# Decoder layer on one core: fp16 pairs for every projection, q and k transposed by DMA, and a new order of work on each engine

## The reference

```python
# attention: B 32, T 112, M 256, H 8 heads, D 128
xn = layernorm(x)
q, k, v = (einsum('bim,mhd->bhid', xn, w) for w in (wq, wk, wv))   # w: 256 x 8 x 128
q, k = rope(rmsnorm(q)), rope(rmsnorm(k))      # rope: [e*cos - o*sin, e*sin + o*cos]
s = einsum('bhid,bhjd->bhij', q, k) / 128      # causal mask, then softmax
x = x + einsum('bhid,hdm->bim', softmax(s) @ v, wo)
# context: both weights are the context itself
x = x + gelu(layernorm(x) @ ctx.T) @ ctx       # 112 x 256 by 256 x 375, and back
# feed-forward, quantised to 8 bits: 256 -> 1024 -> 256
h = relu(quant(quant(layernorm(x)) @ quant(w1).T + quant(b1)))
x = x + h @ quant(w2).T + quant(b2)
```

## Time and profile before

| what | us |
|---|---|
| median of three runs | 731.43 |
| the profiled execution | 730.79 |
| its span (first to last instruction) | 729.1 |
| PE busy | 697.2 (96%) |
| DVE busy | 642.4 (88%) |
| ACT busy | 486.9 (67%) |
| POOL busy | 248.3 (34%) |
| granted TensorE clock, mean | 0.986 of full speed |

### The profile page before, as it was taken

One profiled execution on the slowest core, in us unless ns is written; L12 is line 12 of the kernel. 1 busy time (PEld: TensorE's weight loads), 2 busy tenths in 40 slices (PEclk: granted clock), 3 DMA queues, 4 the chain that ended last, 5 costly groups with the idle time before them and its releaser, 6 DMA issues.

```text
span 729.1 us, 15114 instructions
## 1 busy us (share of the span) xinstructions
PE 697.2 (96%) x5504; PEld 609.9 (84%) x5504; DVE 642.4 (88%) x1232; ACT 486.9 (67%) x1226; POOL 248.3 (34%) x393
## 2 busy tenths in 40 slices
PE   5599999999999999999999999999999999999974
PEld 4488888888888888888888989889888888888863
DVE  6989999999999999999999999999999999998942
ACT  5667766677766677776667767666777766677742
POOL 1344333433332343333234243333334333433310
PEclk9899999999999999999999999999999999999996
DMA  8501110111111011111111111101111110111100
GB/s 268 204 8 49 49 48 24 54 57 49 55 48 42 26 55 55 48 52 51 32 35 55 55 48 48 52 22 47 55 53 50 48 47 24 54 50 43 49 7 13
DMA packets 23946, 38.86 MB, mean 53 GB/s; under 512 B 2048, under 2 KB 18896, under 8 KB 23664
## 3 DMA queue, kind: packets, MB, share of 16 engines
q1 hardware_dynamic: 23920, 38.51, 17.5%
HBM read 34.84 MB, written 3.67 MB: 53 GB/s over the span
## 4 chain that ended last, share of the span: by engine, by line
PE 89%; DVE 3%; ACT 3%; issue 2%; DMA 2%; SPq 0%; POOL 0%; POOLq 0%; DVEq 0%; ACTq 0%
PE psum L846 34%; PE psum L833 17%; PE psum L874 7%; PE psum L854 6%; PE psum L911 6%; PE psum L920 6%; PE psum L945 4%; PE psum L937 3%; PE psum L881 3%; PE psum L902 2%; DMA w_raw<-in_wv 1%; DMA w_raw<-in_w 1%; ACT qkn L743 1%; PE psum L927 1%; DVE turn_c L492 0%
## 5 line engine op out<-in xcount | busy, mean ns | idle before, releaser
L846 PE MATMUL psum<-wqkv_hi,xnT_hi 128*112 128x512 f32 x384 | 165.1, 430 | 4.8 <-DVE wqkv_lo L433 2.8
L846 PE MATMUL psum<-wqkv_lo,xnT_hi 128*112 128x512 f32 x384 | 152.3, 397 | 0.0
L846 PE MATMUL psum<-wqkv_hi,xnT_lo 128*112 128x512 f32 x384 | 131.4, 396 | 0.0
L697 ACT ACTIVATE sq<-psum 112x1024 f32<-112x1024 f32 x64 | 65.5, 1023 | 79.7 <-PE psum L846 79.7
L344 POOL TENSOR_TENSOR rstd<-ve,nhalf 112x1 f32<-112x1 f32 x96 | 55.4, 578 | 156.0 <-DVE ve L407 151.0
L351 POOL TENSOR_TENSOR rms<-ms,nhalf 112x8 f32<-112x8 f32 x64 | 106.3, 1662 | 5.0
L733 ACT ACTIVATE w_raw<-psum,rden 112x128 f32<-112x128 f32 x256 | 69.5, 384 | 45.7 <-DVE rden L519 45.7
L846 PEld LDWEIGHTS psum<-wqkv_hi,xnT_lo 128*112 128x112 f32 x384 | 67.5, 176 | 22.1
L846 PEld LDWEIGHTS psum<-wqkv_hi,xnT_hi 128*112 128x112 f32 x384 | 68.1, 177 | 21.4 <-issue 3.1
L476 DVE TENSOR_TENSOR turn_c<-psum,cos_t 112x1024 f32<-112x1024 f32 x64 | 78.1, 1220 | 6.2 <-ACT sq L697 5.6
L468 DVE TENSOR_REDUCE ss<-sq 112x4 f32<-112x512 f32 (+1 forms) x95 | 81.9, 862 | 0.0
(11 more groups left out here) (82 smaller groups left out, 1531.4 us busy)
## 6 DMA issues: line engine op xcount, KB each, us to landing
ctx_in<-in_ctx_rows SPq DMA_DIRECT2D x32, 375.0 KB
ctxT<-in_ctx_cols SPq DMA_DIRECT2D x32, 375.0 KB, 6.4
x_in<-in_x SPq DMA_DIRECT2D x32, 112.0 KB, 2.0
out_y<-y_out SPq DMA_DIRECT2D x32, 112.0 KB, 1.9
w_raw<-in_w SPq DMA_DIRECT2D x2, 1024.0 KB, 7.5
w_raw<-in_wq SPq DMA_DIRECT2D x2, 512.0 KB, 4.6
w_raw<-in_wk SPq DMA_DIRECT2D x2, 512.0 KB, 6.3
w_raw<-in_wv SPq DMA_DIRECT2D x2, 512.0 KB, 8.0
```

Of the source, the lines that this page charges most:

```text
L846: last = pe.matmul(ps[:, n, :], left[:, c, :], right[:, c, w, n * BANK:(n + 1) * BANK], start=c == 0 and left is xnT_hi and right is wqkv_ ...
```

## The change

What it does, part by part:

1. **Pairs in fp16.** `wqkv`, `wo16`, `xnT16`, `oT16` and the q/k pairs `qk16` are fp16, high and low. So that the low part keeps its bits, each weight matrix is first scaled by a power of two: at the start ACT sums squares of the weights, TensorE adds them over the partitions (`sum_weights`), POOL takes a root, DVE keeps its exponent; the factor is taken out again in the normalisations and in `y_unit`.
2. **q and k.** ACT scales k (eight instructions of 128 columns into `kn`), rounds it to fp16 (`round_k0`), and DVE takes the rest (`split_k`). For q ACT writes the fp16 high part directly (`round_q0`, `round_q1`), and DVE the low part in eight instructions of 128 columns (`split_q`). SP then issues one DMA transpose for k and one for q, each of 112 x 2048 fp16 (448 KB) from SBUF into SBUF. The 16 TensorE transposes and the four passes that read their results from PSUM are gone.
3. **`turn` for k** is done on GpSimd.
4. **No loop, new orders.** All steps are written out (step -3 to 36). The work of a batch is spread over more steps: k and q in step i, v and scores in i+1, weighing and output projection in i+2, context in i+3 and i+4, feed-forward in i+5. PSUM banks are dealt anew, waits that another wait already covers are left out, and `p_sb`, `on` and `wo_raw` have their own place.

The core of the diff:

```diff
-        wqkv_hi = sb("wqkv_hi", [P, MC, 3, HD], F32R)
-        wqkv_lo = sb("wqkv_lo", [P, MC, 3, HD], F32R)
+        wqkv = sb("wqkv", [P, 2, MC, 3, HD], F16)
+        wo16 = sb("wo16", [P, 2, H, M], F16)
...
-            def transpose_qk(w, j):
-                pe.wait_ge(qk_normed[w], done(j))
-                for h in range(H):
-                    last = pe.transpose((qT_ps, kT_ps)[w][:, h // HH, (h % HH) * T:(h % HH + 1) * T],
-                                        qkn[:, w, h * D:(h + 1) * D], ident[0:T, 0:T])
...
+            def transpose_k(j):
+                sp.wait_ge(k_lo_done, done(j))
+                sp.dma_start_transpose(qkT[:, 1], qk16[:, 1].rearrange("t l n -> t (l n)")).then_inc(kT_landed, 16)
+
+            def transpose_q(j):
+                sp.wait_ge(q_lo_done, done(j))
+                sp.dma_start_transpose(qkT[:, 0], qk16[:, 0].rearrange("t l n -> t (l n)")).then_inc(qT_landed, 16)
...
+            def body(i):                                   # SP
+                a, c, d, h = (Batch(i + 3), Batch(i + 1), Batch(i - 0), Batch(i - 4))
+                if h.inside(B):
+                    store_out(h)
+                if a.inside(B):
+                    load_x(a)
+                if d.inside(B):
+                    load_ctxT(d)
+                if c.inside(B):
+                    ...
+                    transpose_k(c)
+                    transpose_q(c)
+                if d.inside(B):
+                    load_ctx(d)
...
+            def turn_k(j):                                 # GpSimd
+                pool.wait_ge(k_sin_done, done(j))
+                pool.tensor_tensor(turn_c[:, 1, :], turn_c[:, 1, :], turn_s[:, 1, :], ALU.add).then_inc(k_turned, 1)
...
+            def split_k(j):                                # DVE
+                dve.wait_ge(k_hi0_done, done(j))
+                dve.tensor_tensor(qk16[:, 1, 1, :], kn[:, :], qk16[:, 1, 0, :], ALU.subtract).then_inc(k_lo_done, 1)
+            def split_q(j):
+                dve.wait_ge(q_hi1_done, done(j))
+                for h in range(H):
+                    at = slice(h * D, (h + 1) * D)
+                    last = dve.scalar_tensor_tensor(out=qk16[:, 0, 1, at], in0=turn_c[:, 0, at], scalar=rms[:, 0, h:h + 1],
+                                                    in1=qk16[:, 0, 0, at], op0=ALU.mult, op1=ALU.subtract)
...
+            def scores(j):                                 # TensorE
+                pe.wait_ge(qT_landed, landed_once(j))
+                pe.wait_ge(kT_landed, landed_once(j))
+                if j.plus(1).inside(B):
+                    pe.wait_ge(k_sin_done, done(j.plus(1)))
...
+            def hidden_units0(j):
+                if j.plus(3).inside(B):
+                    pe.wait_ge(exp_done, done(j.plus(3)))
...
+            for i in range(-3, B + 5):
+                body(i)
```

More of the change, by code:

```diff
@@ new lines, in residual_out @@
+            def residual_out(j):
+                dve.wait_ge(f2_ready, done(j))
+                if j.has(4):
+                    dve.wait_ge(out_stored[(j.plus(-4)).off % SLOTS], landed(j.plus(-4)))
+                if j.off == B - 1:
+                    dve.wait_ge(x3b_done, done(j))
+                dve.scalar_tensor_tensor(out=y_out[:, j.off % SLOTS, :], in0=f2_ps, scalar=1.0 / (ACT_FRAC * W_FRAC),
+                                         in1=x3b[:, :], op0=ALU.mult, op1=ALU.add).then_inc(out_done, 1)
@@ new lines, in project_out @@
+            def project_out(heads, j, first, last):
+                if is_first(j):
+                    pe.wait_ge(wo_done, 2)
+                for h in heads:
+                    pe.matmul(y_ps, oT16[:, h, :], wo16[:, 0, h, :], start=first and h == heads[0], stop=False)
+                    pe.matmul(y_ps, oT16[:, h, :], wo16[:, 1, h, :], start=False, stop=False)
+                    product = pe.matmul(y_ps, oT16[:, H + h, :], wo16[:, 0, h, :], start=False, stop=last and h == heads[-1])
+                return product
@@ new lines, in ctx_out, with project_v0 @@
+            def ctx_out(j):
+                pe.wait_ge(g_done, done(j))
+                pe.wait_ge(ctx_landed[j.off % SLOTS], landed(j))
+                if j.off == 0:
+                    pe.wait_ge(exp_done, done(j.plus(2)))
+                for c in range(SC):
+                    last = pe.matmul(ctx_ps, g[:, c * T:(c + 1) * T], ctx_in[:, j.off % 2, c, :], start=c == 0, stop=c == SC - 1)
+                last.then_inc(ctxout_ready, 1)
+            def project_v0(j):
+                if j.has(5):
+                    pe.wait_ge(out_done, done(j.plus(-5)))
+                if j.off == 1:
+                    pe.wait_ge(v0_copied, done(j.plus(-1)))
+                project(2, 0, v0_ps, j).then_inc(v0_ready, 1)
@@ L897, in i_first, with project_k @@
[L897 to L903 removed]
+            def project_k(j):
+                pe.wait_ge(xnT_lo_done, done(j))
+                project(1, 0, k_ps[:, 0, :], j)
+                project(1, 1, k_ps[:, 1, :], j).then_inc(k_ready, 1)
@@ L913, in ctx_hidden, with project_out0 @@
                 last.then_inc(h_ready, 1)
-            def ctx_out(j):
-                pe.wait_ge(g_done, done(j))
-                pe.wait_ge(ctx_landed[j.off % SLOTS], landed(j))
-                for c in range(SC):
-                    last = pe.matmul(ctx_ps, g[:, c * T:(c + 1) * T], ctx_in[:, j.off % 2, c, :],
-                                     start=c == 0, stop=c == SC - 1)
-                last.then_inc(ctxout_ready, 1)
+            def project_out0(j):
+                pe.wait_ge(oT0_lo_done, done(j))
+                if j.has(3):
+                    pe.wait_ge(f1_int_done, done(j.plus(-3)))
+                project_out(range(0, 2), j, first=True, last=False).then_inc(y0_added, 1)
             def transpose_xq(j):
```

1278 lines of the change are left out of this document (666 added, 612 removed).

## The result

The changed kernel takes **689.08 us** (median of 4 runs, 688.93 to 690.89); the kernel before took 731.42 us beside it. The ratio is 0.942 [0.9405, 0.9442]: faster by 42 us. I had written 643 us, with 628 to 684 as the range. The direction and the period were right; the time was missed by 46 us, and it lies 5 us above the range.

The account below looks back on a forecast made before the run. TensorE was taken as the bound: 21.39 - 1.47 - 0.85 - 0.32 = 18.75, plus 0.25 for waits, 19.0 us per batch. k of batch 6 at 103, 25 x 19.0 to 578, then 27 and 35.7 gave 643 us; range 628 to 684.

Parts of the forecast that it names:

- Steady period: Middle stretch: 19.0 us per batch, from TensorE's stream of 18.75 plus 0.25 for thin waits.
- GpSimd's part: Turn for k adds 2.35 us per batch on GpSimd, 7.9 to 10.3 us.
- DMA transposes at no cost: Transposes of q and k before the scores: price zero as long as the cover of 7.9 us holds.
- Rival 1: Slow DMA transposes: beyond 4.2 us each, scores wait; 678 us at 5.5; chance 0.11 with a gain, 0.06 slower.
- Drain: From the last batch's scores to the end: 35.7 us, as in the kernel before.
- Fill: Pipeline start: first projection at 13.7, 89 us for the first six steps, k of batch 6 at 103.
- The first projection: Start of the fill: k of batch 0 projected at about 13.7 us, against 8.43 before.
- Steps 1 and 2: Fill, from k of batch 0 to k of batch 2: 15.5 and 12 us.
- Step 3: Fill, from k of batch 2 to k of batch 3: 15 us.
- Steps 4 to 6: Fill, from k of batch 3 to k of batch 6: 12.5, 16 and 18 us.
- Rival 3: GpSimd takes DVE's port while turning k: DVE loses up to 2.35 us per batch, 684 us; chance 0.07.
- Rivals 2 and 4: Thin waits add up, period 20.0, 670 us (0.17); fp16 no faster than fp32r, 675, or code starving an engine (0.03).

Follow-up runs that it names:

- e7: Changed kernel with the keys' rotary sum (turn for k) put back on VectorE instead of GpSimd: 699.49 us, period 19.38.
- e8: Changed kernel with each of the two DMA transposes issued twice, the second into a spare tile, scores waiting for both: 728.48 us.
- e1: Changed kernel with only the load of ident issued second instead of tenth: 679.08 us.
- e4: Changed kernel with ident loaded second and preparation of v's, the output projection's, w1 and w2 weights moved later: 678.89 us.
- e13: Changed kernel, ident second, v's and wo's preparation later, w1 and w2 in batches 2 to 4, two transposed-xn buffers, early projection of k(1): 671.73 us.
- e17: e14 with GpSimd's zeroing of the wo, w1 and w2 tiles moved away from the first normalisation of xn: 664.72 us.
- e15: Changed kernel with a filler add on GpSimd between exponential and mask of batches 0, 1 and 2: 699.30 us.
- e9: Changed kernel, ident second, v's preparation later, w1, w2 and wo pieces put where ScalarE and VectorE had been seen to wait: 677.04 us.
- e14: e13 without preparing wo, w1 and w2, which GpSimd sets to zero at the start (output differs): 669.79 us.
- e18: Changed kernel with the filler add on GpSimd in 21 steady steps, behind the root of x2: 694.65 us, period 19.33.
- e16: Changed kernel with the filler add on GpSimd between exponential and mask in batches 8 to 28: 751.70 us.

## Why the prediction was wrong, point by point

- **Steady period: right.** 19.00 against 19.0, with TensorE at 100% and VectorE at 95%. Inside it two terms were off and cancelled, so the exact hit is luck: TensorE's own stream is 19.0, not 18.75, and the waits I had put at 0.25 cost it nothing, since the loop fits under the stream. Which of the stream's terms is 0.25 short is open; the projections (0.216 us per 512 columns) and the output projection (0.109 per 256) are as I had them.
- **GpSimd's part: right**, and undoing it costs 0.38 us per batch (e7).
- **DMA transposes at no cost: right in price and in cover.** From q's issue to the scores it is 7.6 us, where I had 7.9 from q's pair to the scores; each lands in 4.0 us, which leaves 3.5. Rival 1 needed more than S = 4.2 for one transpose; only the doubled ones, when the scores waited for them (e8), used the cover up. The Trainium skill's 261 GB/s ("DMA: Bandwidth & Descriptors", Latency and other measured facts) would make the 459 kB 1.8 us. The trace does not agree: where transposes stand back to back (e8), each holds the queue for 2.2 to 2.6 us, which as an estimate, if that is the transfer, is 180 to 210 GB/s; the measurement decides.
- **Drain: right** (34.3 against 35.7).
- **Fill: wrong, and all of the miss.** The step that failed is "With the work growing to a full step I get 89 us for the first six", with the "27 us for two steps" behind it, and the first projection at 13.7. That projection is at 28.8, and the six steps took 122.4 us. In four parts:
  1. *The first projection* (+15.1). I counted ScalarE's passes over the weights, not what ScalarE's first instruction waits for. I had read in the earlier trace rows that the kernel before starts at 8.43 and carried that start over, though the diff moves `ident` from second to tenth. e1 brings it from 28.8 to 17.4, and with v's sum behind it (e4) it is at 15.3 (14.4 to 15.5 in all runs with both); the last 1 to 2 us stay open.
  2. *Steps 1 and 2* (+8.4 and +13.5). A part is the preparation of wo, w1 and w2, in the order ahead of batch 0's and 1's own work: with everything moved w(3) comes 18.7 us earlier (e13), ident's 10.8 included; without wo, w1 and w2 at all it is 24.8 us (e17). But even there k(0) to k(2) takes 38.1 us, 10.6 more than I had.
  3. *Step 3* (+3.0), the loop of waits. I had seen that step n+2 needs the exponential of batch n, and priced it at 27 us for two steps. The trace goes round in one step: from k(2) at 78.2 over the split of o, k's sine product, the scores of batch 1 (87.6), exponential, mask, root and the roundings of q and xn to k(3) at 96.2, 18.0 us. e15 lengthened one link of it, on the least busy engine, and the whole length came through and more.
  4. *Steps 4 to 6* (+5.3, +2.2, +1.0), TensorE's own work. I had put these steps at 12.5, 16 and 18 us, with no count behind them; TensorE's stream alone fills 17.5, 18.1 and 19.0 us, though context and feed-forward are not yet all there. In these steps TensorE waits once, for 0.3 us.

  The kernel without wo, w1 and w2 (e17) has steps 3 to 5 at the same 18.0, 17.8 and 18.2 us.
- **Rival 3, GpSimd takes VectorE's port:** not for `turn_k`. Its neighbours on VectorE have one input in PSUM and kept 1.22 and 0.49 us. But the effect is there at other places (below), 1 us in an early step.
- **Rivals 2 and 4:** the period did not grow, and fp16 at 512 columns comes 0.216 us apart.

What stays open: which share of the first two steps is the loop, which the lower clock and which the hold-ups between VectorE and GpSimd. In e9 I took visible idle time for free and was wrong; I did not find out which wait replaced it.

## What to carry to other kernels

Price the fill with the same care as the steady step: follow the first batch through each engine's order, and ask of each first instruction what it waits for. A pipeline's early step is as long as its loop of waits or as the work of its longest engine, whichever is more; count both from rows, for each step with the stages that it has. Test a forecast of "hidden" with a filler at that place; here 1.88 us on a half-idle engine cost 3.0 or 0.33 us per batch, by place alone.

## What was unexpected of the hardware

**VectorE and GpSimd can hold one another up until the other's instruction has ended.** A normalisation of 0.41 us took 5.40 beside three memsets of GpSimd (e14), and 1.57 beside the filler (e18). The reverse stands in the changed kernel itself, at 91 us:

```profile
91.12 1.22 DVE L559 TENSOR_TENSOR turn_c<-turn_c,turn_s 112x1024 f32<-112x1024 f32 x1
```

```profile
91.11 1.28 POOL L365 TENSOR_TENSOR ms<-ss,rms_eps 112x8 f32<-112x8 f32 x1
92.47 1.64 POOL L367 TENSOR_TENSOR rms<-ms,nhalf 112x8 f32<-112x8 f32 x1
```

`ms` over 8 columns takes 0.19 us elsewhere and 1.28 here, until VectorE's sum has ended. In the steady part these two do not meet; in e16 they did (`ms` 1.17). Not every pair is held up: in the steady part the same sum runs inside GpSimd's `rms`, and keeps its 1.22 us in all 32 batches, as `rms` keeps its 1.65 (times on GpSimd are rough in the profile):

```profile
317.56 1.22 DVE L559 TENSOR_TENSOR turn_c<-turn_c,turn_s 112x1024 f32<-112x1024 f32 x1
```

```profile
317.13 1.65 POOL L367 TENSOR_TENSOR rms<-ms,nhalf 112x8 f32<-112x8 f32 x1
```

The Trainium skill ("SBUF — State Buffer", SBUF: two separate sides) has the shared pair of ports as an exclusive lock, against VectorE with two SBUF inputs only where GpSimd's operation reads SBUF, and against a two-port mode always. By that rule, the low parts with two SBUF inputs (2.77 us beside a memset of GpSimd in e14, 2.78 without one in e13) go free, and the trace agrees; the normalisation with one input is held up only if it runs in a two-port mode, which no row names. The sum beside `rms`, with two SBUF inputs on either side, would be held up by it; the trace does not agree.
